# Sorted tiles transposed by VectorE in square blocks instead of by TensorE

## What is computed

```python
x = L0_attn_x                                   # (32, 256, 128)
xn = _layernorm(x, axis=-1)
x = x + attn_ref(xn, ...) + ffn_ref(xn, W1, b1, W2, b2)

# attn_ref
u = x @ W_x.T + b_x;  g = sigmoid(x @ W_g.T + b_g)          # hidden 256
h = conv1d(u, conv_w, 3 taps, per channel) + conv_b
u = u * g + h * (1.0 - g)
dt = clip(softplus(x @ W_dt.T + b_dt).mean(axis=(0, 1)), 0.001, 2.0)
A_d = exp(A * dt);  B_d = (A_d - 1.0) / (A + 1e-06) * B_ssm  # 16 states a channel
new = A_d * carry + B_d * u_t;  y_t = sum_s(new * C_ssm)     # scan over 256 steps
return _layernorm(x + y @ W_out.T + b_out, ln_g, ln_b)

# ffn_ref
h = mod(int(x[:, :2].sum(axis=1)), 8)
sel = [h, (h + 1) % 8]
out = sum over the two e in sel of 0.5 * (relu(x @ W1[e] + b1[e]) @ W2[e] + b2[e])   # 128 -> 512 -> 128
```

## Time and profile before

| | us |
|---|---|
| median of 3 runs | 494.08 |
| lowest and highest | 491.63, 494.71 |
| the profiled execution, its own time | 491.58 |
| its span in the trace | 489.8 |

### The profile page before, as it was taken

How to read it: one execution, slowest core, us unless ns; L and a number is a source line. 1 busy time by engine, 2 the same in 40 slices (tenths; PEclk the granted TensorE clock), 3 DMA queues, 4 the chain that set the end, 5 groups by cost and what they waited for, 6 DMA issues and landing times.

```text
span 489.8 us, 10915 instructions
## 1 busy us (share of the span) xinstructions
PE 423.6 (86%) x3463; PEld 375.1 (77%) x3463; DVE 381.3 (78%) x594; ACT 323.4 (66%) x932; POOL 246.3 (50%) x274
## 2 busy tenths in 40 slices
PE   1056799999889999999999899899999999899940
PEld 1034688887889999999999898799998554488840
DVE  6987677665799999999999889999102369957676
ACT  2685599998767777877655765655566665345770
POOL 4595777777333313222542146653122778877720
PEclk9998999999999999999999999999999999999985
DMA  9999345534211111111211214221111846395634
GB/s 237 261 407 324 123 156 181 170 104 141 70 54 32 44 43 43 39 36 43 80 43 43 84 37 132 72 72 43 43 43 33 216 118 152 58 250 148 203 109 128
DMA packets 81254, 56.53 MB, mean 115 GB/s; under 512 B 6178, under 2 KB 74826, under 8 KB 81226
## 3 DMA queue, kind: packets, MB, share of 16 engines
q1 hardware_dynamic: 75274, 47.27, 32.9%
q0 software_dynamic: 4992, 8.40, 6.1%
q10 hardware_dynamic: 960, 0.52, 0.4%
HBM read 27.99 MB, written 23.99 MB: 106 GB/s over the span
## 4 chain that ended last, share of the span: by engine, by line
issue 32%; PE 27%; DVE 12%; DMA 12%; POOL 11%; ACT 3%; POOLq 1%; DVEq 0%; ACTq 0%; SPq 0%
DMA sorted_tokens<-RA,posi 11%; PE PS L1378 8%; POOL AR L580 5%; POOL sorted_tokens L550 3%; PE PS L1445 3%; PE PS L1442 2%; PE PS L1451 2%; DVE RC L1168 2%; PE PS L1361 2%; PE PS L1363 2%; PE PS L1362 2%; PE PS L1428 2%; DVE RC L856 2%; DVE AR L1182 2%; PE PS L1421 1%
## 5 line engine op out<-in xcount | busy, mean ns | idle before, releaser
L1378 PE MATMUL PS<-AR 128*128 128x128 f32 x1184 | 138.5, 275 | 2.3 <-ACT AR L747 2.3
L1378 PEld LDWEIGHTS PS<-AR 128*128 128x128 f32 x1184 | 135.1, 192 | 2.7 <-ACT AR L747 2.7
L747 ACT ACTIVATE AR<-PS,VC 128x256 f32<-128x256 f32 x296 | 112.3, 491 | 10.0 <-PE PS L1363 10.0
L1361 PE MATMUL PS<-XT,RR 128*128 128x256 f32 x296 | 86.2, 291 | 6.5 <-POOL RR L576 3.5
L1363 PE MATMUL PS<-XT,RR 128*128 128x256 f32 x296 | 82.8, 280 | 0.0
L1362 PE MATMUL PS<-XT,RR 128*128 128x256 f32 x296 | 82.5, 279 | 0.0
L556 POOL TENSOR_TENSOR XT<-XTF,XT 128x256 fp32r<-128x256 f32 x37 | 33.3, 900 | 97.8 <-ACT XT L720 97.8
L550 POOL DMA_INDIRECT sorted_tokens<-RA,posi x64 | 61.8, 966 | 23.3 <-issue 13.3
L756 ACT ACTIVATE AR<-PS 128x128 f32<-128x128 f32 x74 | 16.5, 275 | 71.5 <-PE PS L1378 67.8
L580 POOL TENSOR_TENSOR AR<-AR,b2p 128x256 f32<-128x256 f32 x37 | 35.2, 953 | 55.9 <-ACT AR L756 55.6
L1361 PEld LDWEIGHTS PS<-XT,RR 128*128 128x128 f32 x296 | 55.8, 188 | 7.9 <-POOL RR L576 3.9
(11 more groups left out here) (235 smaller groups left out, 875.4 us busy)
## 6 DMA issues: line engine op xcount, KB each, us to landing
sorted_tokens<-RC SPq DMA_DIRECT2D x8, 640.0 KB, 6.7
AR<-sorted_tokens SPq DMA_DIRECT2D x39, 128.0 KB, 2.1
sorted_outputs<-AR SPq DMA_DIRECT2D x37, 128.0 KB, 1.8
RA<-in_L_attn_x_dram SPq DMA_DIRECT2D x8, 512.0 KB, 8.2
AR<-RA SPq DMA_DIRECT2D x16, 256.0 KB, 2.4
normalised_tokens<-RA SPq DMA_DIRECT2D x16, 256.0 KB
RB<-normalised_tokens SPq DMA_DIRECT2D x8, 512.0 KB, 6.1
AR<-in_L_ffn_W_dram SPq DMA_DIRECT2D x15, 256.0 KB, 3.5
```

The source lines that it names most:

```text
L747: nc.scalar.activation(HID[n][:, k, :], ps[2 * n + k // 2][:, (k % 2) * FT:(k % 2 + 1) * FT], ACT.Relu, bias=B1C[:, e, k:k + 1]).then_inc( ...
L1361: T.matmul(bank, W1h[slot][:, w], XT[:, 0:FT], start=True, stop=False)
L1378: ins = T.matmul(ps[5 + h][:, 0:D], HID[n][:, k, h * P:(h + 1) * P], W2S[slot][:, k, :], start=(n == 0 and k == 0), stop=(n == 1 and k == ...
```

## The change

1. **Who transposes the sorted tiles.** PE's `transpose_tile` is gone. A sorted tile is loaded by four DMAs of 32 partitions (`load_tile`), each partition taking 8 runs of 32 numbers (128 bytes), and one DVE instruction transposes it in blocks of 32 x 32 from `XSIN` to `XTF`, which now has two halves. `tiles_to(n)` puts these instructions, with their waits for the load and for the low half of two tiles before, at fixed places of DVE's list: tile 0 before `step(0, 7)`, tile 1 after `step(1, 7)`, 23 among the gate pieces, 12 in the rest, and then on to `NTT` = `MAXT` + 4 = 43. Where there are fewer real tiles, SP and POOL bump the semaphores for the rest, after the last output was stored.
2. **ACT and POOL.** ACT makes one copy (the high half, from `XTF`) in place of two. POOL makes the low half of tile `i + 1` at the start of iteration `i`, tile 1's too. ACT's two exponentials move from the start of group 2 to tile 25, and each signals for itself.
3. **Chunks.** `xin` is gone: PE transposes `XN` itself, and all the stores of normalised tokens stand in one SP loop, each after its chunk's transposition. The zero tile has 8 rows in place of 10 (13 fills in place of 10), and ACT no longer waits for the fills; SP does, ahead of its loads of W2.
4. **Matrices.** `INTRA` is half as large, and the three memsets become 24 of 512 columns.
5. **Tail.** All gathers are plain ones, `add_x` serves all eight batches, and a batch from the fourth on is gathered when the `add_x` four before it is done. `VG`, the pieces scaled on DVE, loses two of six.

The diff, cut to its core:

```diff
-        XTF = sb("XTF", [P, FT])
+        XTF = sb("XTF", [P, 2 * FT])
+        NTT = MAXT + 4
+        TEXP = 25
-        xin = [AR[:, s * CH:(s + 1) * CH].rearrange("p (t d) -> p t d", d=D) for s in range(2)]
+        ZERO = AR[:, 0:2 * CH]
-        XSIN = AR[:, 8 * CH:8 * CH + FT].rearrange("p (h d) -> p h d", h=FH)
+        XSIN = AR[:, 8 * CH:8 * CH + FT].rearrange("p (k a) -> p k a", a=Q)
-        VG = (1, 3, 5, 9, 13, 15)
+        VG = (1, 3, 13, 15)
-        xs_v = xs_dram.rearrange("(t h p) d -> t p h d", h=FH, p=P)
+        xs_v = xs_dram.rearrange("(t k b) (q a) -> q t b k a", k=FT // Q, b=Q, q=NQ)
...
         @block.sync
-            with sp.Fori(1, NCH // 2) as i:
+            with sp.Fori(0, NCH // 2) as i:
                 for s in range(2):
-                    sp.wait_ge(s_xt[s], i)
-                    sp.dma_start(xin[s], XN[:, bass.ds((i * 2 + s) * TPC, TPC), :]).then_inc(s_xin[s], 16)
+                    sp.wait_ge(s_xt[s], i + 1)
                     sp.dma_start(xn_v[:, bass.ds((i * 2 + s) * TPC, TPC), :], XN[:, bass.ds((i * 2 + s) * TPC, TPC), :]
                                  ).then_inc(s_xnd, 16)
...
+            def load_tile(t):
+                for q in range(NQ):
+                    part = xs_v[q][t] if isinstance(t, int) else xs_v[q][bass.ds(t, 1)].rearrange("o b k a -> b (o k) a")
+                    sp.dma_start(XSIN[Q * q:Q * q + Q], part).then_inc(s_xs, 16)
...
             sp.wait_ge(s_yst, bounds[E] * 16 + 16)
             sp.sem_inc(s_step2, 1)
+            with sp.Fori(bounds[E] + 2, NTT) as i:
+                sp.wait_ge(s_tt, i)
+                sp.sem_inc(s_xs, 16 * NQ)
+            sp.wait_ge(s_tt, NTT)
             sp.wait_ge(s_mat, 1)
...
         @block.gpsimd
                 with pool.Fori(bounds[g], bounds[g + 1]) as i:
+                    low_part(i + 1)
                     pool.wait_ge(s_ysb, i + 2)
                     nc.gpsimd.tensor_tensor(YSB, YSB, b2p..., ALU.add).then_inc(s_yad, 1)
-                    low_part(i + 2)
...
+            with pool.Fori(bounds[E] + 1, NTT - 1) as i:
+                pool.wait_ge(s_tt, i + 2)
+                pool.sem_inc(s_xlo, 1)
+            pool.wait_ge(s_tt, NTT)
             pool.wait_ge(s_yst, bounds[E] * 16 + 16)
...
         @block.vector
+            def tiles_to(n):
+                for i in range(done[0], min(n, NTT)):
+                    dve.wait_ge(s_xs, 16 * NQ * (i + 1))
+                    if i >= 2:
+                        dve.wait_ge(s_xlo, i - 1)
+                    V.transpose(XTF[:, i % 2 * FT:(i % 2 + 1) * FT].rearrange("p (k b) -> p k b", b=Q), XSIN).then_inc(s_tt, 1)
+                    done[0] = i + 1
...
+            tiles_to(1)
             step(0, NCH // 2 - 1)
             step(1, NCH // 2 - 1, last=True)
+            tiles_to(2)
...
-            dve.wait_ge(s_ws, 2)
-            low_tile(1)
...
+                    slot = 2 * (hb * NGATE + n)
+                    tiles_to(2 + (23 * slot + 23) // 32)
...
+                    tiles_to(2 + (23 * slot + 46) // 32)
...
             link(V.tensor_tensor(A32[:, :], AP2[:, 0, :], AP2[:, 1, :], ALU.add))
+            tiles_to(NTT)
             dve.wait_ge(s_re[0], bounds[E] * KB)
...
-                if q >= DPB and (q - DPB) % 3 == 0 and (q - DPB) // 3 < NPL:
-                    add_x((q - DPB) // 3)
+                if q in (DPB - 2, DPB + 2, DPB + 5):
+                    add_x((q - DPB + 2) // 3)
...
+                if g == 2:
+                    add_x(3)
+                if g in (3, 7, 11):
+                    add_x(g // 4 + 4)
                 if g + 1 == NT // 4:
+                    scale_gain(13)
                     gain(NB8 - 2)
+                    add_x(NB8 - 1)
...
-            add_x(NB8 - 2)
-            add_x(NB8 - 1)
```

## The result

The changed kernel takes 556.99 us (median of 4, 555.61 to 559.26) against 493.76 (4 runs); the ratio is 1.129, with a 95% interval of 1.126 to 1.133. The forecast was 512, its range 499 to 527. The direction was right and the size was not: +63 us where +19 was forecast. Two executions, one of the run e6 (750.13 us) and one of the kernel before beside e10 (879.09 us), fell in a slower state of the chip, and no median or ratio in this document rests on them.

A forecast was written before the change was run, and what follows sets the result against it. PE bounds the expert stage now, with DVE nearly full; after the change DVE's list with load waits was to bound it. 21.6 + 1.7 - 2.7 - 1.1 = +19.5 on 491.6 gives 511.1, plus 1: 512 us, range 499 to 527.

The forecast's parts named there:

- ACT's exponentials ... move to tile 25, where PE may wait for DVE anyway: Expert stage: exponentials that held PE about 2 us near 280 move to where PE may wait anyway.
- DVE's transposition: Expert stage: 256 columns take 0.52 us on DVE, bounds 0.45 to 0.65; 36 of them 18.7 us.
- DVE's list as the bound: Expert stage: DVE's list with its load waits ends at 381 us against 344.2, and PE ends at 386.5.
- DVE's load waits: Expert stage: DVE waits for single-buffered tile loads, about 6 us in the gate stage and about 10 later.
- PE's gain of 8 us: Expert stage: 37 tiles without PE's transposition save 0.22 us each, if PE stays the bound.
- The front: Before the expert stage: tile 0's load waits behind chunk 15's store, so both engines enter the tiles 7 us late.
- The turn: Before stage 4: four missing tiles at 0.9 to 1.0 us and SP's signal put s_mat 9.5 us behind PE's end.
- Stage 4: Stage 4 and tail: +1.7 for half rate, -2.7 for add_x leaving the end, -1.1 for its earlier places.
- rival (d): Tail: add_x waits for gathers and POOL for add_x, +5 on the forecast, 517 us; chance 5%.
- (a): Whole kernel: it works as meant, DVE's slack takes in the transpositions, about 483 us; chance 5%.
- (b): Expert stage: PE stays the bound, only late start and turn cost, 495 to 500 us; chance 22%.
- (c): Expert stage: loads in 128-byte runs bound it, landing at 3.3 us, 525 us in all; chance 18%.

The follow-up runs named there:

- e6: Against e5: SP's and POOL's bumps for the missing tiles stand ahead of their waits for the last tile; 630.39 us, 0.988 of the kernel before.
- e10: The same kernel as e7, run again; 617.90 us, 0.968 of the kernel before.
- r2: The changed kernel itself, run again beside the later runs; 688.87 us, 1.076 of the kernel before.
- e1: Against the changed kernel: one line reloads the sigmoid tables at the end of ACT's branch for tile 25; 649.90 us, 1.015 of the kernel before.
- e3: Against the kernel before: only the two exponentials and their table load move into a branch for tile 25; 680.71 us, 1.063 of it.
- r1: The kernel before, unchanged, traced again beside the later runs; span 640.8 us.
- e4: The same kernel as e2, run again; 644.02 us, 1.006 of the kernel before.
- e5: Against e4: SP's chunk loop ends with chunk 13 and tile 0 is loaded before the last two stores; 632.52 us, 0.989 of the kernel before.
- e8: Against e6: DVE makes tile 1's low half and signals s_mat before the missing tiles; 630.17 us, 0.987 of the kernel before.
- e2: Against e1: one load of the logarithm and exponential tables on ACT ahead of stage 4; 1.007 of the kernel before.
- e7: Against the changed kernel: PE transposes the sorted tiles again, parts 1 and 2 undone; 619.91 us, 0.970 of the kernel before.

## Why the prediction was wrong, point by point

- **The step that failed: "ACT's exponentials ... move to tile 25, where PE may wait for DVE anyway".** The move was priced at nothing, as two activations and one table load in another place. The branch around them cost a load ahead of relu, gate and output copy in each of the first 16 tiles and one in each later tile, 38 to 39 us of path in the expert stage (r2 against e1, e3 against r1), and in the tail something from 0 to 4 that the scatter hides. Without it the median would come to 556.99 - 39.3, that is 518 or up to 4 less (an estimate from the later runs), against the 512 forecast and inside its range. These loads stood in ACT's compiled order, which can be read without a run. The orders shown ahead of the forecast are those of DVE and SP, and not ACT's.
- **DVE's transposition**: 0.445 us (0.52 taken, bounds 0.45 to 0.65); 43 of them are 19.1 us. Slightly under the low end, right in kind.
- **DVE's list as the bound**: half wrong, and the right length is in part luck. With the tables mended the expert stage takes 260.4 to 262.9 us; the forecast, from about 126 (tile 0, 7 to 8 late) to 386.5, had 260. But PE was busy 85.3 of 87 us in e6 from 213 to 300, with DVE busy 79.9, and lost 14.2 us in five waits for low halves in the whole stage, 7.1 of them for tile 2. DVE did not pace it throughout. DVE's load waits in e4 were 30.9 us, of which 6.9 for tiles 37 and 38 behind the last matrix, so 24 where 16 were forecast. PE's gain of 8 us is in there and is lost: PE idles 16.8 us of e6's expert stage against 8.4 of r1's, and its granted clock there is 0.97 against 0.99.
- **The front**: the chain through SP was right (8.4 us from store to load, DVE standing 13.0, PE 10.1 for 11), and e5 shows it to be worth 10 to 12 us. (Before, the store at 100.43 was issued by 100.87, not 101.1, so those 8.4 were 8.6.) The chain started 4.5 us later than forecast, since what was gained in the chunks went into a longer stall at the new code at 50.87 and half rate behind it. That is a mis-sized term: +13.0 to the first tile, where 7 to 8 were meant.
- **The turn**: 7.5 us for 9.5; the missing tiles follow each other in 0.60 us, not 0.9 to 1.0. Right in mechanism, as e8 shows (1.2 left), but taking it out did not shorten e8 measurably against e6.
- **Stage 4**: +2.8 us for -2.1. With the ten loads taken out it would be -1.4 to +1.4, by e2 and e4. The gathers had stayed hidden in the forecast; whether `add_x` still costs, rival (d), was not told apart; in the later runs the kernels with the changed tail have the shorter stage 4.
- **Rivals.** (a) fell as argued. (b), PE as the bound with late start and turn, has the better account of e6 from 213 us on, but not its short waits. (c), the 128-byte loads: the median landing is 1.8 us, not 3.3, and e1 and e4 keep these loads and reach 260.4 and 262.9 us, so it was wrong. The Trainium skill, DMA: Bandwidth & Descriptors (Specifications), gives 512 bytes as the least transfer for full rate; with 32 KB a load no run here shows what that costs in rate, and the landings show no harm. The other rule, the Trainium skill, VectorE: DVE Perf Modes (Rules for kernel authors), would leave a 128x128 transposition to TensorE; e7 and e10 agree with it: 0.21 us of PE's path a tile was the cheaper price.

## What to carry to other kernels

A long wait of one engine on a single-buffered load can mean that the loop is slow and not the load: find what the load itself took before blaming it. Where one engine is 97% busy and the other is the bound, moving 0.2 us of overlapped work for 0.45 of serial work needs slack where the work lands, in each tile, and not at the end of a list.

## What the runs showed of the hardware

- `ACT_TABLE_LOAD` takes 1.283 us, in the mean of each group of the 84, and the next activation starts right behind it (206.87 + 1.28, then 208.16).
- The same kernel took 494 us in the first runs and 640 on each of four chips later, with an expert stage of 255.8 and 257.6 us, and with the rest of the difference in the two stages in which POOL's indirect DMAs run (PE busy 11.8 of 60 us from 60 to 120, and 59.7 in the first trace). The cause is open.
- A load of 32 KB in runs of 128 bytes landed in 1.8 us (median of 156), one of 128 KB in runs of 512 bytes in 2.1 (37). Size and length of run differ together.
- One DVE transposition of 128x256 fp32 in blocks of 32 x 32 took 0.445 us (43 times).
